# Mean squares of all norms by one product with a 128x128 matrix of 1/128, roots on whole tiles, and a new table of places

## What is computed

```python
def _layernorm(x, axis=-1, eps=1e-05):
    m = jnp.mean(x, axis=axis, keepdims=True)
    v = jnp.var(x, axis=axis, keepdims=True)
    return (x - m) / jnp.sqrt(v + eps)
...
def ffn_layer(x, g, bln, W1, b1, W2, b2):
    mu = x.mean(-1, keepdims=True)
    var = ((x - mu) ** 2).mean(-1, keepdims=True)
    xn = (x - mu) / jnp.sqrt(var + 1e-05) * g + bln
    hg = xn @ W1 + b1
    a, gate = jnp.split(hg, 2, -1)
    return a * jax.nn.gelu(gate, approximate=False) @ W2 + b2
```

## Time and profile before

| | us |
|---|---|
| median of 3 runs | 3816.9 (3813.14 to 3818.65) |
| the profiled execution's own time | 3809.55 |
| its span, first to last instruction | 3807.8 |
| PE busy | 3533.7 (93%) |
| DVE busy | 2700.3 (71%) |
| ACT busy | 2553.1 (67%) |
| POOL busy | 2025.9 (53%) |
| mean granted TensorE clock | 0.985 of full speed |

### The profile page before, as it was taken

The page is one execution under the profiler, slowest core; times in us unless marked ns, Lnnn a source line. Parts: engine busy times, 40 slices in busy tenths (PEclk is TensorE's granted clock), DMA queues, the critical chain, the costliest instruction groups (busy, mean ns, idle before and its releaser), DMA issues.

```text
span 3807.8 us, 149416 instructions
## 1 busy us (share of the span) xinstructions
PE 3533.7 (93%) x65288; PEld 2266.8 (60%) x65288; DVE 2700.3 (71%) x3599; ACT 2553.1 (67%) x5965; POOL 2025.9 (53%) x1564
## 2 busy tenths in 40 slices
PE   8999997899999999999999999999999999999997
PEld 4545543566666666666666666666666666666664
DVE  4565664777777777777777777777777777777762
ACT  5656663667676767676767776767676767677773
POOL 0000000866666666666666666666666666666551
PEclk9999998899999999999999999999999999999997
DMA  1000001433334333333333333333333333333330
GB/s 49 6 6 6 9 4 31 149 122 114 122 126 132 119 121 119 128 127 129 119 120 120 132 128 123 113 121 128 134 116 123 119 125 122 130 118 122 126 111 26
DMA packets 222761, 389.70 MB, mean 102 GB/s; under 512 B 63774, under 2 KB 101916, under 8 KB 221980
## 3 DMA queue, kind: packets, MB, share of 16 engines
q1 hardware_dynamic: 195792, 363.63, 27.8%
q10 hardware_dynamic: 26316, 16.52, 1.5%
HBM read 124.14 MB, written 7.34 MB: 35 GB/s over the span
## 4 chain that ended last, share of the span: by engine, by line
PE 65%; DVE 16%; ACT 7%; issue 5%; DMA 3%; SPq 2%; POOL 2%; ACTq 0%; POOLq 0%; DVEq 0%
PE PS L484 64%; ACT SC L1221 4%; DVE TPB L908 4%; DVE MX L932 3%; DMA RB<-root_scratch 2%; DVE SM L943 2%; ACT AOT L1234 1%; DVE PX L954 1%; DVE VAR L973 1%; POOL K L1314 1%; DVE H L982 1%; DVE PP L953 1%; DVE NV L923 1%; ACT XCH L1092 1%; DMA PP<-PX 1%
## 5 line engine op out<-in xcount | busy, mean ns | idle before, releaser
L908 DVE SCALAR_TENSOR_TENSOR TPB<-PS,VEC,C 128x1024 f32<-128x1024 f32 x768 | 963.3, 1265 | 106.0 <-ACT SX L1197 99.0
L1221 ACT ACTIVATE SC<-PS,BQ,RQ 128x64 f32<-128x64 f32 x3072 | 966.1, 430 | 29.2 <-DVE BQ L937 28.4
L1197 ACT ACTIVATE SX<-PS 128x512 f32<-128x512 f32 x768 | 476.6, 629 | 366.5 <-PE PS L484 363.3
L1314 POOL TENSOR_TENSOR K<-K,RB 128x512 f32<-128x512 f32 x384 | 492.4, 1282 | 300.3 <-DMA RB<-root_scratch 300.3
L1332 POOL TENSOR_TENSOR Q<-TPB,TR 128x512 f32<-128x512 f32 x384 | 491.5, 1280 | 248.1 <-DMA TR<-TPB 230.5
L484 PEld LDWEIGHTS PS<-PP,VV 32*64 32x64 f32 x24576 | 433.7, 133 | 298.1 <-issue 245.2
L484 PE MATMUL PS<-PP,VV 32*64 32x64 f32 (+1 forms) x24576 | 540.6, 223 | 38.3 <-DMA PP<-PX 23.2
L1337 POOL TENSOR_TENSOR SC<-SC,RC 128x1024 f32<-128x1024 f32 x192 | 365.8, 1905 | 332.5 <-DVE RC L945 331.4
L1332 POOL TENSOR_TENSOR K<-TPB,TR 128x512 f32<-128x512 f32 x384 | 493.6, 1285 | 0.0
L943 DVE TENSOR_REDUCE SM<-SC 128x16 f32<-128x1024 f32 x192 | 234.2, 1220 | 336.1 <-ACT SC L1221 335.0
L484 PE MATMUL PS<-LXH,LH 128*128 128x512 f32 x768 | 370.9, 483 | 62.9 <-DVE TPB L908 56.0
(11 more groups left out here) (168 smaller groups left out, 6208.3 us busy)
## 6 DMA issues: line engine op xcount, KB each, us to landing
TR<-TPB SPq DMA_DIRECT2D x768, 256.0 KB
RB<-root_scratch SPq DMA_DIRECT2D x768, 128.0 KB, 3.1
PP<-PX SPq DMA_DIRECT2D x192, 192.0 KB, 2.6
WS<-in_wqkv ACTq DMA_DIRECT2D x72, 128.0 KB, 2.6
PP<-PX SPq DMA_DIRECT2D x192, 48.0 KB, 2.4
root_scratch<-NV SPq DMA_DIRECT2D x384, 8.0 KB
LO<-in_wo ACTq DMA_DIRECT2D x6, 512.0 KB, 3.8
T<-in_x SPq DMA_DIRECT2D x8, 256.0 KB, 3.0
```

Source lines behind the costliest of these rows:

```text
L908: e.scalar_tensor_tensor(TPB[:, n % 3:4 + n % 2:3 + n % 2 - n % 3, w, :], g, VEC[:, l, 9 + w:10 + w], C[:, at:at + 1024].rearrange("p (o c ...
L1197: e.activation(SX[i % 3][:, :], bk("PJ", key)[:, :], ACT.Square).then_inc(sem["pj_act"], 1)
L1221: p = e.activation(SC[m % 2][:, g, :, :].rearrange("p x k -> p (x k)"), bank[s][:, at:at + 64], ACT.Exp, bias=BQ[m % 2][:, g:g + 1], scale ...
L1314: e.tensor_tensor(dst, dst, RB[n % 2][:, :], ALU.mult).then_inc(sem["pr_pool"], 1)
```

## The change

`om`, the constant of 1/128, grows from one column to 128, so that F2 and N2 are one product each (128x512 out, in fp32), whose result holds the variance of each token on every partition. `spread`, N4 and F3 on PE go. Ln and Exp on ACT now read and write whole 128x512 tiles, with epsilon as Ln's bias, and DVE's add of epsilon goes. The Newton step (N3, F2n) is three `scalar_tensor_tensor` on 128x512: the first reads the variance in PSUM, the other two read SBUF alone. The multiplication with the root (F3, AX, AZ, AW, E2) now reads the root from SBUF, no more from PSUM. The squares and the roots of "in", "mid" and "x" have tiles of their own (NQ, NZ), "end" has EZ, the FFN FX. F2's bank is kept until the first of the three DVE steps has read it; F3 takes no bank any more. And every number of PLACE is a new one.

The diff, cut to its core:

```diff
 PLACE = {
-    "S1": 0.070, "MX": 0.204, "S3": (0.520, 0.817, 1.345, 1.440), "SU": 1.481, "NP": 2.090, "TT": 2.494,
-    "PX": 2.428, "PV": (3.608, 3.721, 4.542, 5.121), "PVn": 5.291, "PJ": (-7.527, -7.038),
...
-    "VP": -0.654, "VC": -0.535, "WO": (12.494, 12.664, 12.743, 12.755), "F1": 13.903, "F2": 14.160,
-    "F2n": 14.420, "F3": 15.011, "F3l": 15.140, "TB": (15.648, 16.315), "F4": (15.746, 15.781, 15.832),
...
+    "S1": 0.054, "MX": 0.183, "S3": (0.569, 0.730, 0.996, 1.176), "SU": 1.449, "NP": 1.857, "TT": 2.464,
+    "PX": 2.428, "PV": (4.415, 5.084, 5.540, 5.561), "PVn": 6.115, "PJ": (-7.657, -7.129),
...
+    "VP": -0.715, "VC": -0.554, "WO": (12.685, 12.742, 12.744, 12.783), "F1": 13.969, "F2": 14.230,
+    "F2n": 14.644, "F3": 15.362, "F3l": 15.127, "TB": (16.095, 16.439), "F4": (16.103, 16.123, 16.200),
...
-    def spread(kind, b):
-        rel, per = {"in": ("in_dve", 1), "mid": ("mid_dve", 1), "x": ("xa_dve", 2), "end": ("end_dve", 1)}[kind]
-        o.put("N4", kind, b, banks=[(None, rel, 1, 1)])
-        o.keep(o.bank["N4", (kind, b), 0], rel, per * (b + 1))
+    def squares(kind, b):
+        o.put("N2", kind, b, banks=[(None, kind + "_root", 3, 1)])
+        o.keep(o.bank["N2", (kind, b), 0], kind + "_root", 3 * b + 1)
...
-        at(z + P["F2"], group, "F2", u, "f2_dve", 4 * u + 1)
+        at(z + P["F2"], group, "F2", u, "f2_dve", 3 * u + 1)
         at(z + P["F2n"], o.put, "F2n", u)
-        at(z + P["F3"], group, "F3", u, "f3_dve", u + 1)
+        at(z + P["F3"], o.put, "F3", u)
...
-                    for k in range(4):
-                        p = mm(bk(st, key)[:, k:k + 1], H[0][:, 128 * k:128 * k + 128], cn("om"))
-                    p.then_inc(sem["f2_pe"], 1)
-                elif st == "F3":
-                    u, = key
-                    on.wait_ge("f2_dve", 4 * u + 4)
-                    free(on, st, key)
-                    spread(bk(st, key), VAR[:, 3, :]).then_inc(sem["f3_pe"], 1)
+                    mm(bk(st, key)[:, :], cn("om"), H[0][:, :]).then_inc(sem["f2_pe"], 1)
...
+            def rsqrt(v, u, x, step, done, r):
+                on.wait_ge(step, 2 * r + 2)
+                e.scalar_tensor_tensor(u, v, EPS, x, ALU.add, ALU.mult).then_inc(sem[done], 1)
+                on.wait_ge(done, 3 * r + 1)
+                e.scalar_tensor_tensor(u, u, -0.5, x, ALU.mult, ALU.mult).then_inc(sem[done], 1)
+                on.wait_ge(done, 3 * r + 2)
+                e.scalar_tensor_tensor(x, u, 1.5, x, ALU.add, ALU.mult).then_inc(sem[done], 1)
...
-                    on.wait_ge("f3_pe", u + 1)
-                    e.tensor_tensor(H[2][:, :], H[1][:, :], bk(st, key)[:, :], ALU.mult).then_inc(sem["f3_dve"], 1)
+                    on.wait_ge("f2_dve", 3 * u + 3)
+                    e.tensor_tensor(H[2][:, :], H[1][:, :], FX[:, :], ALU.mult).then_inc(sem["f3_dve"], 1)
...
-                    ln_exp(VAR[:, 2, :], VAR[:, 0, :], VAR[:, 1, :], -0.5, "f2_act", u + 1)
+                    if u:
+                        on.wait_ge("f3_dve", u)
+                    on.wait_ge("f2_pe", u + 1)
+                    ln_exp(H[0][:, :], bk(st, key)[:, :], FX[:, :], -0.5, "f2_act", u + 1, cn("hilo")[:, 3:4])
```

114 lines of the change are left out of this document (38 added, 76 removed), and 15 rows, old and new, of the table PLACE.

## The result

| | before | after |
|---|---|---|
| median us (4 runs each) | 3817.78 (3813.14 to 3825.01) | 3670.3 (3663.41 to 3678.27) |
| the profiled execution's own time | 3809.55 | 3674.32 |
| span | 3807.8 | 3672.5 |
| mean granted TensorE clock | 0.985 | 0.986 |

The changed kernel takes 0.9613 of the time of before (95% interval 0.9586 to 0.964): 3.9% faster. Between the profiled executions the difference is 135.2 us, where the sum gave 76.7.

A forecast was written before the change was run, and what follows sets the result against it. It took PE as the bound, busy for 93% of the span; -49.3 - 39.4 - 8 - 10 - 38 + 62 + 6 = -76.7 us from the median 3816.9 gave 3740 us, range 3690 to 3825.

The forecast's parts named there:

- Terms 1 and 2: Norms on PE: one fp32 product each replaces the one-column and spreading products; 49.3 us (FFN) and 39.4 us (others) saved.
- Term 3: PE's 15.2 us idle for the root ahead of the spreading products goes with them; taken as -8 us.
- Term 4: PE's 23.2 us wait for the shifting DMA before the products with the values shrinks, as they come later; -10 us.
- Term 5: PE's 49.0 us wait inside F4 for a rotary product shrinks with S1 put ahead of F4; -38 us.
- Term 6: The longer root on DVE delays the next rotary product, so PE waits 1.3 us more a unit; +62 us.
- 7, ACT: Exp and Ln on ACT take 68 us more in all, but stand before the root, behind the transposes anyway; nothing.
- term 9: At the kernel's end nothing runs beside the norms: some 2.3 us more in each of three chained norms; +6 us.
- Rival A: The lump decides: the root's SBUF-only steps stand for POOL, PE waits 3.0 us more a unit; slower, 3860 us; chance 0.17.
- Rival B: The lump is hidden altogether and the waits for PX and inside F4 go entirely; 3654 us; chance 0.10.
- T + 7.1 is past T + 5.95: T ends S1's products; the rotary product ends at T + 7.1 us without standing, PE wants its bank at T + 5.95.
- term 8: First stage: 24 x some 2.4 us more work on DVE and ACT, busy for some 60%, costs nothing.
- the last check: The forecast is wrong if, among other signs, the first stage is not shorter by some 30 us.

## Why the prediction was wrong: its own steps

| term | forecast us | measured us |
|---|---|---|
| 1 and 2, products of the norms | -88.7 | -63 in PE's busy time (new order, old against new operations) |
| 3, wait for the root N | -8 | -14 |
| 4, wait for PX | -10 | -23 |
| 5, wait inside F4 | -38 | -40 |
| 6, DVE's lump | +62 | -8, all other waits for the rotary product and the root's bank |
| 7, ACT | 0 | 0 |
| 9, the end | +6 | +0.4 (from F4's last product on: 21.1 us before, 21.5 after) |
| not in the sum: PE's work, by the new order alone | | about -20 |
| not in the sum: POOL K | | -11 |
| not in the sum: "issue" | | +29 |
| not in the sum: all other waits, of both signs | | about +14 |

Without term 9's +0.4, which is a stretch of time and holds waits that are in the other rows, the measured terms add up to about -136 us, where the spans differ by 135. The two figures of PE's work are differences of its busy totals (-83 us together), the others of waits (-53 us together). The forecast for the same two was -88.7 and +12: the work was nearly right by luck, as the product terms were 26 us too large and an effect of the order, 20 us, was not in the sum; the waiting was wrong by 65 us.

**Term 6 is the step that failed**: 70 us between forecast and outcome, where the whole miss is 58.5 (the other terms' misses, of both signs, make up the rest). Its walk through one unit came out: the root ended at T + 5.8, the rotary product at T + 7.1, both at the walk's early end, and PE came at T + 6.4. There was some luck in that: the root began at T + 3.25, 0.45 us sooner than I had it, and its second step stood 0.49 us. But the walk's result, a wait of 1.1 us or more where 0.37 us had been, was priced against one row of before, and the sum for the whole kernel was made as if all other waits for L908 stayed. They did not. Outside F4, PE waited 126.5 - 49.0 = 77.5 us for L908 before; in the changed kernel it waits 58.3 - 0.2 = 58.1, and 11.3 for L747: 8 us less in all, in spite of the lump. In the unit shown before there was a second wait of 0.83 us for the next rotary product, two microseconds behind the one that I priced; in the unit of after none follows the 0.65 us. That the places do this by themselves shows with the old operations in the new order: there PE waits 65.1 us for rotary products in all, 46.0 of it in the old F3, where it was 127.4 before. That the lump as it stands is hidden was then shown by taking 78 us of it away, for 4 to 12 us.

What hides it is the order: MX is no longer behind the add (it starts at T + 0.04, where it was T + 1.3), the root is where ACT's result is ready (moved ahead, it costs 1.5%), and F2's bank is wanted one projection later (moved back, it costs 2.8%). The first of these was argued from the unit shown and not tried by itself. The last of these is not in my working at all. The term asked when DVE would be late and for which rotary product, and of the bank of the mean squares it said in term 3 only that some other pieces stand in front of its next user. Moved back, this place costs more than the root's own, the only other one that was tried in the new order.

**Rival A** did not come, since the steps hardly stand for POOL. With the old places the new operations give 3866 us, and rival A said 3860; that is a coincidence, as its mechanism is not what PE waits for there. The Trainium skill's rule ("SBUF — State Buffer", "Who interferes with whom") lets a step with two SBUF inputs block until a GpSimd instruction that reads SBUF, and that started first, has ended. As I took it for rival A, nearly every such step would stand, for over a microsecond; the measured means are 0.22, 0.01 and 0.3 us. Single ones do stand (the longest L948 is 1787 ns, and L749 took 1.18 us in the unit shown), so the trace doesn't speak against the rule: it tells what can happen, not how often.

**Rival B** ("the order pays in full") is the case that came, with its mechanism: the lump is hidden, the waits of terms 4 and 5 go. That its 3654 us lie only 16 from the median is in part luck: its product terms were 26 us too large, and the new order's work (-20) and "issue" (+29) were not in it. I gave it 0.10, because T + 7.1 is past T + 5.95. That argument was true and did not decide: a wait of 0.65 us there is less than what the new order takes from the waits on both sides of it.

**Terms 1 and 2** were too large. The new rows are even cheaper than forecast: `H,C` 49.6, `NQ,C` 28.3, `ES,C` 9.8 us, for 54.0 and 38.3 together; by rows alone all the norm products fell from 273.3 to 175.0 us, by 98.3. But between the two kernels with the new order the rows of the norm products that changed fall by 91 us, and PE's own total, where both traces lack the same records, by 62.8. The rest is booked on other rows. `LH,LXH`, which follows the new product, shows 0.80 us in the timeline instead of 0.50, and its row goes from 187.6 to 202.0 us, which is 48 x 0.30; `LXH,LH` goes from 362.0 to 368.2, and why isn't shown. I had added rows whose records overlap.

**Term 5** held in size, but not as an independent term: moved alone, F4's place takes the 49 us of waiting away and gives nothing (0.9996). **Term 4** was mis-sized: the wait went entirely, from 23.2 us to nothing; moved alone it too gives nothing, and costs 0.7%. **Term 3** went beyond its forecast and within its bounds: the 15.2 us ahead of `C,N` are gone with the product, and the other norm rows gave 1.5 us back.

**The first stage** did not do what term 8 and the last check had it do. Up to the first product of F4 (801.5 us before, 789.0 after) it is 12.5 us shorter, not some 30; with the new operations in the old order it is 21 us longer, with the old operations in the new order 0.8 longer. PE is busy for 735.1 us of it before and 713.9 after, 21.1 less and not 29.6, by the overlap as above; and it idles 75.1 us instead of 66.4. With the new operations in the old order PE is busy for 719.4 and idles 103.1, with the 23.2 us for the root's first step among it. So term 8's "nothing" holds only with the new places; with the old ones the longer root, which now stands behind ACT's Exp on whole tiles and keeps one of two banks, costs more than the products save there.

## What to carry to other kernels

In a kernel whose engines run fixed queues and share a ring of banks, a change of places can't be priced move by move: each of the moves tried alone gave nothing or cost up to 6%, and all together gave 2%. A longer instruction lump on an engine that is not the bound can cost next to nothing or about its full length, depending on what stands behind it and which turn of the ring is waiting for it; so work out for the kept bank who takes it next, and when, before pricing the lump. And a saving in busy time should be read from the engine's total in two traces with the same records, not from the rows' sums, where pipelined products overlap. When a variant is slower, look first whether PE waits more or works longer: several runs here are slower with no more waiting, or with less.

## What the runs showed that I had not expected

DVE's standing hardly grew with the work that could stand. It moved. (The profile names no cause; that it is POOL for which short steps stand is the prediction's reading of their lengths.) BQ (L915, 128x16), the first short step behind MX, takes 694 ns on the mean now, where it took 510 before, 35 us more in 192 of them. The three steps on NV (128x128) went from 192.5 to 183.6 us in all. And the root stood some 49 us before (70.5 us for 144 steps that take about 0.15 us when nothing holds them, the minimum of the earlier trace rows) and stands, with L948, some 25 now. Together that is about as much as before.

The order changed the length of products too. `AOT,LO` takes 342.4 us for 351.2, and 343.0 with the old operations in the new order, 352.4 with the new ones in the old order. In PE's timeline the first product behind a piece of another kind takes 0.50 us and the next ones 0.39 to 0.40; in the new table the four places of WO lie closer together (12.685 to 12.783 for 12.494 to 12.755), so its sixteen products are cut up less. With the FFN's places alone, WO's among them, the row is at 343.5 us too.

The granted clock was lower in several slower orders: 0.986 of full speed in the changed kernel, 0.975 to 0.978 in three of its variants (table above), 0.961 with the FFN's places alone, 0.965 and 0.960 with the late root and with RQ first in the old order, and the same to within 0.005 in every execution of each. In the last three the products with the values (`PP,VV`) take 551 to 558 us for 537 to 541, so that a part of what those orders cost, some 14 to 21 us in this row, comes with the clock and not with waiting. By stretch of 500 us the kernel with the FFN's places was granted 0.97 throughout the second stage, with PE busy 448 to 454 of 500 us:

```profile
750.00:1250.00 500.00, 448.07 (x9470) 301.13 (x9476) 347.24 (x440) 328.91 (x816) 303.46 (x237) 0.97 0.34 116
```

The new operations in the old order have PE busy for 453 to 458 of 500 us in the same stretches, and a granted clock of 1.00.

Left open are which part of the new order, beyond RQ and the root's place, makes it work as a whole; what in an order lowers the granted clock; and why "issue" waits rose from 22 to 49 us. The missing records don't explain that: with F4's place alone the same records are missing, and "issue" is 22.5 us.
